# P7 added to the copy of P5 by VectorE straight from PSUM, in place of a ScalarE copy and a GpSimd addition, in a factorization-machine layer built on Strassen's scheme

## The reference, cut to what matters

```python
# x: 2048 x 512, beta: 1024 x 8 x 512, W: 1024 x 512, b: 1024
s = jnp.einsum('bn,hln->bhl', x, beta)
ssq = jnp.einsum('bn,hln->bhl', x * x, beta * beta)
fm = 0.5 * jnp.sum(s * s - ssq, axis=-1)
y = fm + x @ W.T + b
```

## Time and profile before

| | us |
|---|---|
| three runs, median | 802.9 (802.03 to 802.95) |
| the profiled execution | 802.24 |
| its span, first to last instruction | 800.5 |
| TensorE busy in it | 776.9 (97%) |
| VectorE busy | 557.1 (70%) |
| ScalarE busy | 410.4 (51%) |
| GpSimd busy | 374.2 (47%) |
| mean granted TensorE clock | 0.994 of full speed |

### The profile page before, as it was taken

One profiled execution on the slowest core, in us unless ns is written; L12 is line 12 of the kernel. 1 busy time (PEld: TensorE's weight loads), 2 busy tenths in 40 slices (PEclk: granted clock), 3 DMA queues, 4 the chain that ended last, 5 costly groups with the idle time before them and its releaser, 6 DMA issues. The chain is left out here.

```text
span 800.5 us, 9817 instructions
## 1 busy us (share of the span) xinstructions
PE 776.9 (97%) x3382; PEld 635.8 (79%) x3382; DVE 557.1 (70%) x642; ACT 410.4 (51%) x564; POOL 374.2 (47%) x332
## 2 busy tenths in 40 slices
PE   8998999899999999999999999999999999997998
PEld 5876878678888888888888888888888888876886
DVE  6699457985766566666666765766577656688784
ACT  5464445465555555555546555655555544562330
POOL 0153256435553555465446545654555365523333
PEclk9999999999999999999999999999999999998999
DMA  8596764156633463456146614651663256449633
GB/s 337 190 404 252 270 202 160 36 203 243 211 119 109 165 219 112 141 186 229 37 145 211 211 33 156 233 183 30 226 218 119 59 209 216 162 176 347 221 138 143
DMA packets 66738, 145.35 MB, mean 182 GB/s; under 512 B 4864, under 2 KB 41728, under 8 KB 64384
## 3 DMA queue, kind: packets, MB, share of 16 engines
q1 hardware_dynamic: 66688, 144.72, 51.1%
HBM read 102.76 MB, written 41.94 MB: 181 GB/s over the span
## 5 line engine op out<-in xcount | busy, mean ns | idle before, releaser
L432 PE MATMUL bank<-t_hi,s_hi 128*128 128x512 f32 x1116 | 437.9, 392 | 18.3 <-DVE s_lo L736 6.6
L436 PE MATMUL bank<-t_lo,s_hi 128*128 128x512 f32 x1124 | 438.9, 390 | 0.2 <-DVE t_lo L675 0.2
L438 PE MATMUL bank<-t_hi,s_lo 128*128 128x512 f32 x1116 | 435.4, 390 | 0.0
L432 PEld LDWEIGHTS bank<-t_hi,s_hi 128*128 128x128 f32 x1116 | 210.5, 189 | 68.2 <-DVE s_lo L736 8.6
L436 PEld LDWEIGHTS bank<-t_lo,s_hi 128*128 128x128 f32 x1124 | 211.9, 189 | 44.1 <-DVE t_lo L675 0.7
L438 PEld LDWEIGHTS bank<-t_hi,s_lo 128*128 128x128 f32 x1116 | 210.4, 189 | 44.0
L910 POOL TENSOR_TENSOR r<-r 128x512 f32<-128x512 f32 x70 | 107.7, 1538 | 226.3 <-ACT r L591 226.3
L779 DVE TENSOR_REDUCE sums<-cs 128x128 f32<-128x1024 f32 x128 | 155.5, 1215 | 76.6 <-ACT cs L610 71.8
L763 DVE TENSOR_TENSOR cs<-bank,r 128x512 f32<-128x512 f32 x70 | 48.3, 691 | 90.7 <-PE bank L438 87.9
L914 POOL TENSOR_TENSOR cs<-r 128x512 f32<-128x512 f32 x70 | 91.1, 1301 | 27.4 <-issue 18.3
L873 POOL TENSOR_TENSOR t_lo_in<-t_lo_in 128x1024 f32<-128x1024 f32 x36 | 87.1, 2421 | 30.0 <-PE bank L438 29.7
(11 more groups left out here) (52 smaller groups left out, 352.4 us busy)
## 6 DMA issues: line engine op xcount, KB each, us to landing
s_hi<-s_hi_kept SPq DMA_DIRECT2D x30, 896.0 KB, 5.2
s_lo<-s_lo_kept SPq DMA_DIRECT2D x30, 896.0 KB, 6.9
t_lo_in<-beta_p SPq DMA_DIRECT2D x16, 1024.0 KB, 7.2
s_lo_in<-x_p SPq DMA_DIRECT2D x16, 512.0 KB, 4.5
acc_kept<-cs SPq DMA_DIRECT2D x16, 512.0 KB, 7.7
acc<-acc_kept SPq DMA_DIRECT2D x64, 128.0 KB, 5.4
acc_kept<-acc SPq DMA_DIRECT2D x64, 128.0 KB, 1.8
s_hi_kept<-s_hi SPq DMA_DIRECT2D x8, 896.0 KB, 3.7
```

The lines of the kernel that those rows point to most:

```text
L432: nc.tensor.matmul(to, s_hi[:, slot, s_op, cols], hi[:, k, :], start=start, stop=False, skip_group_check=True)
L436: nc.tensor.matmul(to, s_hi[:, slot, s_op, cols], lo[:, k, :], start=False, stop=False, skip_group_check=True)
L438: return nc.tensor.matmul(to, s_lo[:, slot, s_op, cols], hi[:, k, :], start=False, stop=stop, skip_group_check=True)
```

## The change

ScalarE no longer copies P7 to r7, and GpSimd no longer adds r7 to r5. VectorE adds BANK_D to r5, in place, right after r2; it waits for P7 and for the copy of P5. TensorE's wait before P4 is now for this addition. GpSimd's C22 waits for it as before for its own addition. The tile r7 is gone; the warm-up matmuls read a tile of their own.

```diff
-        r7 = sb("r7", [P, COLS])
+        idle = sb("idle", [P, 256])
...
-        warm_up = r7[:, 0:256].bitcast(bf16)
+        warm_up = idle[:, :].bitcast(bf16)
...
                 if g < FIRST_Q:
-                    pe.wait_ge(r7_copied, count(g))
+                    pe.wait_ge(r57_added, count(g))
...
-            def copy_r7(g):
-                act.wait_ge(p7_made, count(g))
-                if g > DIRECT:
-                    act.wait_ge(r57_added, count(g - 1))
-                nc.scalar.copy(r7[:, :], bank(g, BANK_D)).then_inc(r7_copied, 1)
...
                 copy_r5(g)
-                copy_r7(g)
...
+            def add_r57(g):
+                dve.wait_ge(p7_made, count(g))
+                dve.wait_ge(r5_copied, count(g))
+                nc.vector.tensor_tensor(r5[:, :], bank(g, BANK_D), r5[:, :], ALU.add).then_inc(r57_added, 1)
...
                 add_r2(g)
+                add_r57(g)
                 if g + 2 in PREPARED:
...
-                pool.wait_ge(r5_copied, count(g))
-                pool.wait_ge(r7_copied, count(g))
-                nc.gpsimd.tensor_tensor(r5[:, :], r5[:, :], r7[:, :], ALU.add).then_inc(r57_added, 1)
                 pool.wait_ge(r57_added, count(g))
```

More of the change, by code:

```diff
@@ L194, in fm_layer @@
         r5_copied = sem("r5_copied")
-        r7_copied = sem("r7_copied")
         r2_added = sem("r2_added")
```

## The result

| | before | changed |
|---|---|---|
| median of 4 runs, us | 802.76 (802.03 to 802.95) | 812.88 (811.89 to 813.67) |
| profiled execution, us | 802.24 | 813.67 |
| its span, us | 800.5 | 811.9 |
| mean granted TensorE clock | 0.994 | 0.992 |

The ratio is 1.0127, 95% interval 1.011 to 1.0145: 10 us slower. The forecast was 811.3 us, slower. Three single executions at a low clock or far off the rest (e3_double 977.63 us at a mean clock of 0.751, the profiled one of e4_free 1307.87 us at 0.557, one of the kernel before 1586.07 us) are left out of every ratio.

The account below looks back on a forecast made before the run. TensorE, busy 776.9 of 800.5 us, was taken to set the time. Terms of 7.2 + 2.4 - 0.9 = +8.7 us on the profiled 802.24 gave 810.9, put on the middle of the runs 811.3 us; range 806.5 to 816.5.

Parts of the forecast that it names:

- the deadline at P4: In 24 ordinary groups (18 to 63), VectorE's new addition ends after P4's weight load is due, 0.41 us late.
- (a): Rival: weights load during the wait at P4, so only the matmul is late, 0.18 us x 24; 808.4 us, 8 in 100.
- (b): Rival: the new addition starts after the end of L757, 0.47 instead of 0.30 us per group; 816.2 us, 12 in 100.
- (d): Rival: work leaves ScalarE and GpSimd, fits into VectorE's idle time, nothing else is felt; 802.9 us, 2 in 100.
- (e): Rival: the short pauses lower the granted clock each time, 24 times some 2 us; 850 us or more, 2 in 100.
- (c): Rival, not slower: VectorE's chain runs 0.41 us earlier without L910, P4 is not held; 800.5 to 804.5 us, 6 in 100.
- Its own signs: Expected in the changed profile: 24 holds, late groups 9.82 us apart, group 16 2.4 us late, no r5 wait in group 9.
- The ordinary groups: P4 held in 24 groups of 18 to 63, 0.30 us each: 7.2 us (bounds 4.3 to 11.3).
- The lateness minus 0.12: At P4: a product whose weight load comes late by x is delayed by x - 0.12 us; 0.41 late gives 0.30.
- Groups 2 to 15: Where TensorE waits for VectorE: +1.3 and +1.1, so group 16 starts 2.4 us late (bounds 0 to 5).
- The end: Groups 70 to 72: VectorE's chain gains more than its two additions of 0.61 us cost; -0.9 us (bounds -1.5 to +1.2).
- The relief: Without GpSimd's L910, VectorE gains 1.1 us in group 4, 1.0 in 13, about 1 in 14, 2 at the end.

Follow-up runs that it names:

- e3_double: Changed kernel with one more VectorE addition (P7 + r5 into a spare tile) ahead of the one P4 waits for; ratio 1.0411.
- e4_free: Kernel before with one more VectorE addition per group (P6 + r1 into a spare tile, ahead of r2) that no engine waits for; 805.04 us.
- e1_swap: Changed kernel with the two VectorE additions in the other order, P7 to r5 first, then r2; 801.51 us.
- e6_free2: Same kernel as e4_free, a single run for its trace; 806.56 us.
- e7_nopool: Kernel before without GpSimd's addition of r7 (C22 of groups 2 to 71 leaves P7 out), nothing put in; 793.69 us.
- e9_early: e1_swap with the addition of P7 alone ahead of the step and low part of x in groups 4, 5, 13 and 14; 802.73 us.
- e10_early2: As e9_early, with the early addition in groups 13 and 14 only; 801.77 us.
- e8_first: e1_swap's order, with both additions ahead of the step and low part of x in all groups but a pass's first; 818.09 us.

## Why the prediction was right, and where its terms were off

**Right: the deadline at P4.** From group 16 to 70 the holds come in the 24 groups that were named and in none of the others. Start and duration of the addition (0.08 us before r2's end, 0.68 us), the load held to 0.05 us after the addition's end and the matmul starting with it are as in the changed trace. e1_swap, e3_double and e6_free2 show it three ways: less lateness, no loss; more lateness, as much more loss; the same work without a waiter, no loss. Of the rivals, (a), a load ahead of its wait, is out: the load started with the release all 34 times. The Trainium skill's reordering of weight loads (TensorE: Matmul & The Clock Gate, "Architectural detail: the array is 16× 32×32, not 1× 128×128") doesn't reach past this wait. (b) is out by the start of the addition, (d) by the 34 holds, (e) since the 0.3 us holds left the clock alone. (c), VectorE's chain earlier by 0.4 us, did not happen by itself; e1_swap made it happen by order, and then the time was indeed not above that of before.

**Its own signs.** The time from a late group to the next was 9.83 to 9.87 us in most cases (9.82 forecast), and the long cases of the split of x (3.13 us) and of the update (1.39 us) are gone. But others failed: group 16 came 4.5 us late and not 2.4, the wait for r5 in group 9 did not go, and the granted clock fell three times before the last instructions (at 74.5, 156.5 and 736.7 us) where it had fallen twice. The prediction had named a further fall as a sign that it was wrong; that fall belongs to the term of groups 2 to 15, not to the deadline at P4.

**The ordinary groups, 7.2 forecast, 8.3 measured.** The lateness minus 0.12 was right for the pause (0.28 to 0.29 us in 20 groups). The rule left out that the matmuls after a release don't follow at 0.227 us at once: in group 29 they start at 316.97, 317.30 and 317.54, the last gap 0.24. With such small rests a group costs 0.31 to 0.35 us. Three groups cost more, 18, 35 and 53 (0.53, 0.45 and 0.43 us), because there the update, which has two inputs in SBUF, ran beside GpSimd's addition of the bias and took 0.64, 0.53 and 0.51 us instead of 0.43. In group 18:

```profile
205.63 0.88 POOL L904 TENSOR_TENSOR acc<-acc,bias_all 128x128 f32<-128x128 f32 x2 [2.27 <-DMA acc<-acc_kept]
206.16 0.64 DVE L782 SCALAR_TENSOR_TENSOR acc<-sums,acc 128x256 f32<-128x256 f32 x1
```

In a late group VectorE's chain has no slack left, so this 0.2 us goes straight to TensorE. The mean of the 24 is 0.34 us.

**Groups 2 to 15, 2.4 forecast, 4.9 measured.** This is the term that was mis-sized, though within its bound of 5. (Its first part adds up to 1.4 and not 1.3: -0.1, 0.9 and twice 0.3.) Three parts. Groups 3 to 5 came to 2.5 us where I had 1.0: the pause of 2.8 us at P4 of group 5 that I had found did lower the clock, which stood only in the bound. In group 9 the wait of P3 for P5's copy shrank from 1.1 to 0.4 us instead of vanishing, and P4 was held 1.3 instead of 0.9: with TensorE later by 2.0 us GpSimd's and ScalarE's work came later too. What comes first is GpSimd's bias for group 8, which waits for a DMA load of acc. That load was issued 2.1 us later (97.51 against 95.45), the bias started 2.7 us later (108.05 against 105.37), and so C22 of group 8, ahead of the copy of P5 in ScalarE's queue, came at 108.89 instead of 107.57 although L910 is gone. In the changed kernel:

```profile
108.05 0.88 POOL L904 TENSOR_TENSOR acc<-acc,bias_all 128x128 f32<-128x128 f32 x2 [14.61 <-DMA acc<-acc_kept]
108.89 1.28 POOL L909 TENSOR_TENSOR cs<-r 128x512 f32<-128x512 f32 x1
```

The forecast had counted TensorE's delay and the end of this wait both in full. From group 13 to 16 it was 1.25 us, forecast 1.1. VectorE's update had indeed lost its long form; the addition of P6 in group 13 still moved by 1.8 us, from 155.45 to 157.24, and not by nothing, because the groups ahead of it were 3.2 us late and not 1.3.

**The end, -0.9 forecast, -1.3 measured.** The mechanism was right: P4 of group 71 was held 1.9 us and TensorE's next pause, at P3 of group 72, was 3.9 us instead of the 5.5 of the earlier trace rows.

**The relief.** I took it as 1 us here and there, some 5 us in all. e7_nopool measured GpSimd's addition in the old kernel at 9 us, of which some 2 are the fall of the clock in group 14 that it brings about. I had judged it by the stretched instructions in a few rows; the pauses that follow from them, and the clock behind these, weigh more. By an estimate from the table, if the changed kernel has the whole relief (6.9 us in groups 3 to 15 and 2.3 at the end), its additions cost 11.8 and 1.0 us there, and only the difference, 3.6 us, was seen. Both were forecast much smaller.

**What was luck.** The traces differ by 11.4 us where 8.7 were forecast, the medians by 10.1, since the traced execution of the changed kernel is the slowest of its four. And by the estimate above the relief and the cost in the first and last groups were both taken too small and largely made up for one another; that this stretch came out only 2 us off is luck.

## What to carry to other kernels

When work moves to another engine, don't ask whether that engine has idle time, but when its result is due, and what stands ahead of it in its queue in each kind of group: 0.61 us of VectorE work added to each of 70 groups where nobody waited for it cost 2.8 us, in the trace none of it in groups 16 to 71, and 0.4 us of lateness in 24 groups cost 8. Then look whether the order can be changed before giving the move up: the same two additions the other way round took 11 us off. And an elementwise addition on GpSimd is not free for VectorE where VectorE is late, even if the GpSimd engine is half idle.

## What the runs showed of the hardware

- A held product costs the lateness of its weight load minus 0.12 us, plus some 0.04 us: the matmuls after a release come at 0.23 to 0.24 us before they are back at 0.227. Two lengths of hold, 0.28 and 0.88 us, agree.
- After a pause of TensorE of 2 to 3 us the granted clock may fall or not. I counted the delays of over 1 us from group 2 on in eleven traces (all but e4_free's; a delay is the gap between two matmul starts less 0.227 us, plus the 0.11 us by which the next one comes late). The clock fell after none of those below 2.0 us. Of 16 between 2.0 and 2.9 us it fell after 7 and stayed after 9, and twice the two outcomes lie side by side: 2.17 us and no fall, 2.15 and a fall in the same place of the same code; 2.81 and a fall, 2.80 and none at P1 of group 14 in e9_early and e10_early2. At all 21 of 3.2 us and more it fell, during the pause or behind it. A fall covered 5 to 13 matmuls at 0.43 instead of 0.23 us. What decides between 2 and 3 us stays open. The spread of 3 us between runs of one kernel goes with the clock: e1_swap's two executions at a mean of 0.996 took 799.82 and 800.36 us, the three at 0.991 took 802.12 to 803.07. That falls behind such pauses make this difference is likely, but only one of these executions has a trace.
- VectorE's additions with one input in PSUM and one in SBUF took 0.67 to 0.69 us each time. The new one hardly ever met GpSimd at work (once in 70), but C12 did in 58 of its 70 groups in the changed kernel, and P6 + r1 in 35 of 78 in the kernel before (counting more than 0.2 us side by side). Operations with two inputs in SBUF were stretched beside GpSimd, by 1.1 us in the earlier trace rows and 2.1 us in e8_first. The lock of the port pair that the Trainium skill describes (SBUF — State Buffer, "SBUF: two separate sides") fits both.
